# Forty-eight identity transposes on TensorE at the begin of each of the four norms of a language-model tower

## The reference, cut to what matters

```python
h = tok(x, ...)                                    # n-gram embedding of 2 x 1024 tokens, 128 features
h = h + retention(layernorm(h), ...)               # 8 heads of 16
h = h + experts(layernorm(h), ...)                 # 8 experts, 2 used, all computed
h = h + attention(layernorm(h), ...)               # 8 heads of 128
h = h + latent(layernorm(h), ...)                  # 128 query heads against 100 latent rows
return h

def layernorm(x): return (x - mean(x)) / sqrt(var(x) + 1e-5)      # over the 128 features
```

## Time and profile before

| what | us |
|---|---|
| median of three runs | 3082.61 |
| the three runs | 3079.25, 3082.61, 5605.95 |
| the profiled execution's own time | 3107.84 |
| its span, first to last instruction | 3106.0 |
| mean granted TensorE clock over the span | 0.948 |

### The profile page before, as it was taken

One profiled execution on the slowest core, in us unless ns is written; L12 is line 12 of the kernel. 1 busy time (PEld: TensorE's weight loads), 2 busy tenths in 40 slices (PEclk: granted clock), 3 DMA queues, 4 the chain that ended last, 5 costly groups with the idle time before them and its releaser, 6 DMA issues.

```text
span 3106.0 us, 44621 instructions
## 1 busy us (share of the span) xinstructions
PE 2780.7 (90%) x14652; PEld 2264.8 (73%) x14652; DVE 2293.7 (74%) x4039; ACT 1750.1 (56%) x3398; POOL 2094.3 (67%) x1520
## 2 busy tenths in 40 slices
PE   0569989696999999779999999999999999999996
PEld 0437666595888888568888888888777787788875
DVE  1459989535666666568888888888888888888875
ACT  0269978334656656435555655555555555555553
POOL 5369978103777777527777777777777776777763
PEclk7589999798999999879999999999999999999997
DMA  1011100000000000100111111011010100111100
GB/s 46 22 35 27 27 21 16 28 1 28 1 1 1 1 1 1 63 17 33 44 34 44 34 37 39 34 44 45 32 34 32 44 32 33 46 37 34 45 19 7
DMA packets 44693, 87.01 MB, mean 28 GB/s; under 512 B 10677, under 2 KB 24781, under 8 KB 43825
## 3 DMA queue, kind: packets, MB, share of 16 engines
q1 hardware_dynamic: 42928, 81.00, 8.0%
q0 software_dynamic: 1536, 3.15, 0.4%
HBM read 64.44 MB, written 1.05 MB: 21 GB/s over the span
## 4 chain that ended last, share of the span: by engine, by line
PE 39%; DVE 6%; POOL 6%; issue 4%; ACT 0%; POOLq 0%; ACTq 0%; DVEq 0%
PE lat_ps_h L2173 15%; PE lat_ps_z L2184 8%; PE lat_ps_s L2123 7%; PE lat_ps_t L2152 6%; POOL lat_zz L1800 3%; POOL lat_wq L1763 2%; PE lat_ps_s L2139 2%; PE lat_ps_s L2130 2%; DVE lat_wq_sum L1857 1%; DVE latm_sc L1837 1%; DVE latm_top L1832 1%; DVE latm_attT L1852 1%; DVE latm_tot L1844 1%; POOL latm_att L1787 0%; PE lat_ps_s L2206 0%
## 5 line engine op out<-in xcount | busy, mean ns | idle before, releaser
L1787 POOL TENSOR_TENSOR latm_att<-latm_sc,latm_tot 128x500 f32<-128x500 f32 (+1 forms) x416 | 421.4, 1013 | 460.6 <-DVE latm_tot L1846 450.1
L2173 PE MATMUL lat_ps_h<-latm_attT,lat_share 125*128 125x512 f32 (+1 forms) x2472 | 681.1, 407 | 34.8 <-DVE latm_attT L1852 31.7
L1800 POOL TENSOR_TENSOR lat_zz<-lat_zz,lat_zsq 128x512 f32<-128x512 f32 x508 | 655.3, 1290 | 20.0 <-ACT lat_zsq L2030 12.7
L2023 ACT CAST latm_attT<-lat_ps_t 125x512 fp32r<-125x512 f32 (+1 forms) x512 | 301.8, 589 | 620.8 <-PE lat_ps_t L2152 620.8
L2173 PEld LDWEIGHTS lat_ps_h<-latm_attT,lat_share 125*128 125x128 f32 (+1 forms) x2472 | 461.7, 189 | 160.5 <-DVE latm_attT L1852 54.8
L2184 PE MATMUL lat_ps_z<-latm_attT,lat_vc 100*128 100x512 f32 x1536 | 485.5, 424 | 0.2 <-ACT lat_zsq L2030 0.2
L995 POOL TENSOR_SCALAR mha_probs<-mha_probs,mha_inv 128x1024 f32<-128x1024 f32 x128 | 364.6, 2849 | 121.7 <-DVE mha_inv L1216 121.5
L1852 DVE TENSOR_TENSOR latm_attT<-lat_ps_t,latm_attT 125x512 fp32r<-125x512 f32 (+1 forms) x512 | 348.5, 681 | 107.3 <-ACT latm_attT L2023 107.0
L2123 PE MATMUL lat_ps_s<-lat_wk,lat_xr 128*128 128x500 f32 (+1 forms) x1248 | 353.0, 392 | 12.3 <-DVE latm_sc L1837 5.5
L457 POOL TENSOR_TENSOR ret_probs<-ret_probs,ret_shared 128x1024 f32<-128x1024 f32 x128 | 306.1, 2425 | 49.3 <-ACT ret_probs L590 49.3
L2152 PEld LDWEIGHTS lat_ps_t<-ident,latm_att 128*125 128x125 f32 (+1 forms) x2048 | 284.2, 175 | 63.7 <-POOL latm_att L1787 16.6
(11 more groups left out here) (366 smaller groups left out, 4812.3 us busy)
## 6 DMA issues: line engine op xcount, KB each, us to landing
lat_w_in<-in_w_fives SPq DMA_DIRECT2D x52, 640.0 KB, 4.2
lat_wq_in<-in_wq_fives SPq DMA_DIRECT2D x52, 320.0 KB, 2.9
lat_share<-lat_share SPq DMA_DIRECT2D x200, 50.0 KB
ret_qk_head<-ret_qk_parts SPq DMA_DIRECT2D x256, 32.0 KB, 2.0
moe_w<-in_W SPq DMA_DIRECT2D x2, 1024.0 KB, 4.8
ret_shared<-in_xpos_q SPq DMA_DIRECT2D x1, 1024.0 KB, 5.6
ret_shared<-in_xpos_k SPq DMA_DIRECT2D x1, 1024.0 KB, 4.8
latw_wkv<-in_Wkv SPq DMA_DIRECT2D x1, 1024.0 KB
```

The lines of the kernel that those rows point to most:

```text
L1787: nc.gpsimd.tensor_tensor(att[:, k % SLOTS].rearrange("p (j l) -> p j l", j=QH)[:, 0:n, 0:L], sc[:, u, 0:n * L].rearrange("p (j l) -> p j ...
L1800: nc.gpsimd.tensor_tensor(dst, dst, zsq[:, n % 2], ALU.add).then_inc(s["zz_added"], 1)
L2173: mm = e.matmul(ps_h[:, f, c, :], share[0:w, q % 2, w_part, cols], attT[0:w, n % 2, a_part], start=(n % NS in (0, QH) and (a_part, w_part) ...
```

## The change

A new method `warm` issues 48 transposes of the identity by the identity, into the four quarters of the first PSUM bank that the turns use. It has no wait and no semaphore. It is called once in each phase that has a norm: in `Norm.tensor`, ahead of the first turn, for `retention`, `attention` and `latent`, and in `experts`, which has a loop of its own for the turns, ahead of that loop. In the source of the changed kernel the new transposes are L202, the turns are L209, and later lines move by four to six.

```diff
@@ class Norm @@
+    def warm(self, e):
+        for n in range(48):
+            e.transpose(self.psT[:, 0, n % 4 * P:(n % 4 + 1) * P], self.ident[:], self.ident[:])
+
     def turn(self, e, g):
         e.wait_ge(self.scaled, START + g + 1)
@@
     def tensor(self, e):
+        self.warm(e)
         for g in range(NT // 4):
             self.turn(e, g)
@@ experts, block.tensor @@
+            norm.warm(e)
             for g in range(NT // 4):
                 norm.turn(e, g)
```

## The result

| | kernel before | changed kernel |
|---|---|---|
| median, us | 3081.46 | 3092.33 |
| lowest, us | 3077.34 | 3090.63 |
| runs | 8 | 8 |
| span of the profiled execution, us | 3106.0 | 3093.4 |
| its mean granted clock | 0.948 | 0.956 |

The ratio is 1.004 with a 95% interval of 1.0029 to 1.0051. The medians differ by 10.9 us; by the ratio the change costs 12.3 us, and by its interval 8.9 to 15.7 us. One of the eight runs of the kernel before took 5605.95 us and is not in the ratio. The forecast was 3093 us, +10.8 us.

A forecast was written before the change was run, and what follows sets the result against it. VectorE and ScalarE were taken to bound the norms of retention and experts, TensorE those of attention and latent. 0 - 1.4 + 5.3 + 6.9 = +10.8 us on the 3082.6 us median gave about 3093 us, range 3083 to 3104 us.

The forecast's parts named there:

- Retention, 0 us: Norm of retention: the 48 transposes run under the 15.7 us in which TensorE waits for VectorE, costing 0 us.
- the 8.3 us of idleness: Retention, between block and first turn: idleness longer than the 4.8 us after which the clock fell, so turns stay slow.
- Experts, -1.4 us: Norm of experts: block ends ahead of the first turn; first turns gain 0.45 us, later work about 1.0 us.
- Attention, +5.3 us: Norm of attention: all 48 run at the high clock behind the folded weights and delay the first turn 5.3 us.
- Latent, +6.9 us: Norm of latent: block starting at the low clock takes 7.4 us ahead of the turns, less 0.5 us regained.
- the 0.5 us: Latent, behind the block: first four turns at the high clock end 0.45 us earlier, taken as 0.5 us off the delay.
- The sum, +10.8 us: Whole kernel: the four norms' terms, 0 - 1.4 + 5.3 + 6.9 us, added to the median.
- Rival 1: All four norms: the 48 never lift the clock and let it fall; sum +20.0 us, 3103 us; chance 12%.
- Rival 2: The clock, once up, carries through the norms and over the logits; sum +1.9 us, 3085 us; chance 12%.
- Rival 3: Latent: another wait than that for `xT` absorbs the delay; sum +3.9 us, 3086 or 3087 us; chance 8%.
- Rival 4: TensorE's stream is interrupted, by instruction fetching or otherwise; passing 2% needs 0.6 us per open transpose; chance 2%.

The follow-up runs named there:

- all covered: Against the kernel before: 48 transposes in experts, 96 ahead of attention's folded weights, 32 ahead of latent's matmuls on weights, none in retention; 3077.1 against 3081.7 us, ratio 0.9984.
- the last kernel above: 48 transposes in experts, 96 and 32 moved ahead of waits in attention and latent, none in retention, against the kernel before; 3077.1 us, ratio 0.9984.
- retention alone: The 48 transposes in the norm of retention only, against the kernel before; 3082.4 against 3081.6 us, ratio 1.0002.
- the block ahead of the folded weights: Attention's block only, 96 transposes moved to where TensorE waits for GpSimd's centred weights, against the kernel before; 3077.8 against 3081.7 us, ratio 0.9987.
- twice as many: 96 instead of the changed kernel's 48 transposes at each of the four places; 3106.0 us against 3081.7 us for the kernel before, ratio 1.0077.

## Why the prediction held, step by step

**Retention, 0 us: right.** Ratio 1.0002, the turn not moved by 0.01 us, the clock back down before it, as the 8.3 us of idleness had said.

**Experts, -1.4 us: right in kind, too large.** The block was covered (7.10 us of 8.7) and the first turns ran at the high clock, which gave the 0.45 us of ScalarE's earlier start. The other us was to come from a clock that holds for 4 us behind the block. It held 3.3 us (560.8 to 564.1 us) and fell just before the first logits began, so they gained nothing. In the kernel with all covered the same block ended 8.22 us behind VectorE's first instruction, as the clock had risen later in it, the clock held into the logits, and the hidden layer started at 17.19 us, 2.2 us early. Three profiles have this block and give 0.45, 0.45 and 2.2 us at the hidden layer; no run here shows what decides between them.

**Attention, +5.3 us: right.** 5.24 us of block in both profiles that have 48 there. The stage takes 581.4 and 582.6 us in them, and 575.6 to 577.0 us in the five profiles with nothing new in it, 4.4 to 7.0 us less; the start of the folded weights, which wait for GpSimd and its weights' DMA, moves by 1.3 us between profiles.

**Latent, +6.9 us: right.** The block took 7.56 us up to the first turn in the changed kernel, where 7.4 us (7.0 to 7.9) were forecast, and 8.12 us alone, beyond that range, since the clock rose only 5.9 us into it; the 0.5 us came back as forecast, between the first turn and GpSimd's first copy (1.31 us where it was 1.80 us); the stage grew by 6.2 to 7.6 us against the five profiles with nothing new in it, the runs by 6.8 us.

**The sum, +10.8 us against +10.9 us measured,** has some luck in it: `experts` gave a us less than forecast, and by the ratio the change costs 12.3 us, with 8.9 to 15.7 us as its interval. The runs hold the forecast but are not fine enough to confirm its parts to a us; that is done by the traces. The bounds of the sum in the prediction, +7 to +14 us, are narrower than the ends it gave term by term (it takes -3 us for `experts` where its own paragraph has -4.2, and 7.4 us for `latent` where that has 10.6); the measured cost lies within either.

**Rival 1, that transposes do not lift the clock, fell.** In `retention` and `experts` of the changed kernel nothing but transposes ran, and the windows at 1.00 hold 31 and 32 of these instructions. The Trainium skill's rule in "TensorE: Matmul & The Clock Gate", Part 4, that the high clock does not engage for transposes, does not hold for these fp32 transposes: by it the block of `latent` would have taken 10.6 us, and it took 7.56 us. **Rival 2, a clock that carries through the norms, fell** with the clock of 0.50 from 564.2 to 572.6 us. **Rival 3, a delay absorbed in `latent`, fell** with +6.8 us for that block alone, and with ScalarE's exponentials, which moved by 7.4 us in the changed kernel. **Rival 4,** a far higher price of each transpose, had nothing: 5.24 us for 48 is 0.109 us each, and 10.48 us for 96 the same.

## What to carry to other kernels

Work that was to lift TensorE's clock was free here only where TensorE waited; find the wait that ends last ahead of each place, and put the work before that wait, not behind it. A block of 48 transposes cost 5 to 7 us per norm between the matmuls and the turns; 96 and 32 of them gained some 4 us each ahead of the wait of those matmuls. Size such a block so that it ends as the wait does. What is to profit must follow closely: behind the block in `experts` the clock was down again after 3.3 us. What a block runs over delays the next instruction in full (4.6 us in `experts` with 96). And read the gain at the end of the stage, not at the next instruction: a late loop can take it back.

## What the runs showed of the hardware that was not expected

- TensorE can be busy without a break and have the low clock, in the middle of a dense loop. In `experts` of the last kernel above it fell to 0.50 at 589.4 and again at 596.2 us and came back within 4 us, though PE was 100% busy in both windows. The same happened once in the profiles of retention alone and of the block ahead of the folded weights, and twice with twice as many (one line, one line and two, in this order):

```profile
599.00:602.60 3.60, 3.60 (x18) 3.49 (x17) 0.92 (x3) 0.00 (x0) 0.00 (x0) 0.53 0.00 0
601.90:605.30 3.40, 3.40 (x15) 3.21 (x15) 1.01 (x5) 0.00 (x0) 0.00 (x0) 0.50 0.00 0
595.40:598.90 3.50, 3.50 (x17) 3.36 (x17) 0.90 (x4) 0.00 (x0) 0.00 (x0) 0.52 0.02 5
602.30:605.70 3.40, 3.40 (x17) 3.30 (x16) 0.68 (x2) 0.00 (x0) 0.00 (x0) 0.51 0.00 0
```

  In the other six profiles it did not happen, and the kernel before held 1.00 from 610 to 709 us. The stage's length follows these spells: 134.2 to 134.6 us without one, 136.2 us with one in the two stages that had nothing new, so 1.6 us each. With two it is 139.0 us where the hidden layer started 1.2 us late, and 135.7 us where it started 2.2 us early, in both cases 3.2 us beyond what that start gives. Right ahead of all six spells stand the bias matmuls on 8 rows (587.09 and 594.06 us in the last kernel, 2.05 us for 16), but such a group stands at 618.26 us in the kernel before too, and no fall behind it. So what a high clock gains ahead of this loop can be lost in it, and the runs do not show what decides that.
- The `retention` stage, the same code in most of these kernels, has lengths from 456.6 to 461.0 us. Between 230 and 520 us the profile at 456.6 us has one low spell of the clock, the two at 460.9 and 461.0 us have four each, and most others two; one at 459.2 us has four. Effects of under 3 us drown in scatter of this size, here with ten or more runs of a kernel (four of twice as many).
- The logits, eight columns wide, are not bound by something that the clock leaves alone: eight of their instructions took 0.96 us at the high clock and 1.85 us at the low one.
